# Local attention on one Trainium2 core: whole 128-token transposes replaced by pairs of 64-token ones that share two banks

## What is computed

```python
def attn_layer(x, Wqkv, qs, ksc, Wo):          # 16 heads of width 64, x is 2048 x 128
    q, k, v = heads of x @ Wqkv                # each 2048 x 1024
    q, k = l2norm(q) * qs, l2norm(k) * ksc
    q, k = rotary(q), rotary(k)
    out = local_attention(q, k, v)             # windows of 32 tokens see their own and the one before
    return out @ Wo
for i in range(6):
    x = attn_layer(shift_tokens(x), ...) + x
    x = ffn_layer(shift_tokens(x), ...) + x
```

## Time and profile before

| | |
|---|---|
| device time, median of 3 runs | 5310.74 us (5309.5 to 5312.04) |
| span of the profiled execution | 5297.4 us |
| median of the runs less that span | 13.3 us |
| PE busy, PE weight loads | 4675.9 us, 2897.7 us |
| DVE, ACT, POOL busy | 4003.6 us, 3636.0 us, 2657.4 us |
| mean granted TensorE clock | 0.957 |

### The profile page before, as it was taken

One profiled execution on the slowest core, in us unless ns is written; L12 is line 12 of the kernel. 1 busy time (PEld: TensorE's weight loads), 2 busy tenths in 40 slices (PEclk: granted clock), 3 DMA queues, 4 the chain that ended last, 5 costly groups with the idle time before them and its releaser, 6 DMA issues. The chain is left out here.

```text
span 5297.4 us, 148317 instructions
## 1 busy us (share of the span) xinstructions
PE 4675.9 (88%) x45796; PEld 2897.7 (55%) x45796; DVE 4003.6 (76%) x8097; ACT 3636.0 (69%) x11780; POOL 2657.4 (50%) x2108
## 2 busy tenths in 40 slices
PE   5999999698898998989989767989989989899897
PEld 1333332366565665656656544665656656566565
DVE  7888886587786877868778546878868778687785
ACT  1777777586785876858768514867858778587684
POOL 3000000465665666656656404656656566566564
PEclk6999999899999999999999977999999999999998
DMA  0000000222222222222222302222222222222223
GB/s 13 1 2 1 2 1 1 85 59 72 59 59 77 59 71 60 59 77 59 64 66 60 83 7 85 59 73 59 57 78 59 72 62 57 77 60 69 65 56 93
DMA packets 332305, 288.20 MB, mean 54 GB/s; under 512 B 149102, under 2 KB 290964, under 8 KB 329748
## 3 DMA queue, kind: packets, MB, share of 16 engines
q1 hardware_dynamic: 331028, 281.93, 20.6%
q10 hardware_dynamic: 768, 0.02, 0.0%
HBM read 100.42 MB, written 30.41 MB: 25 GB/s over the span
## 5 line engine op out<-in xcount | busy, mean ns | idle before, releaser
L929 POOL TENSOR_TENSOR g_rn<-g_ss,g_minus_half 128x8 f32<-128x8 f32 x384 | 636.8, 1658 | 299.7 <-DVE g_ss L1077 297.0
L929 POOL TENSOR_TENSOR f_rn<-f_ss,f_minus_half 128x8 f32<-128x8 f32 x384 | 636.8, 1658 | 299.2 <-DVE f_ss L1077 295.9
L425 DVE TENSOR_REDUCE a_maxima<-a_max 128x1 f32<-128x512 f32 x1024 | 651.3, 685 | 148.4 <-PE a_max L539 142.2
L1003 ACT ACTIVATE f_ex<-f_bank,f_nmx 128x96 f32<-128x96 f32 x1536 | 501.5, 338 | 226.8 <-DVE f_nmx L1082 226.8
L1003 ACT ACTIVATE g_ex<-g_bank,g_nmx 128x96 f32<-128x96 f32 x1536 | 501.6, 338 | 226.6 <-DVE g_nmx L1082 226.6
L349 ACT ACTIVATE a_pex<-a_scores 128x512 f32<-128x512 f32 x1024 | 531.7, 607 | 159.6 <-PE a_scores L548 159.6
L934 POOL TENSOR_TENSOR f_qr<-f_t 128x512 f32<-128x512 f32 x384 | 488.4, 1272 | 268.8 <-DVE f_t L1100 268.8
L934 POOL TENSOR_TENSOR g_qr<-g_t 128x512 f32<-128x512 f32 x384 | 488.2, 1271 | 269.0 <-DVE g_t L1100 269.0
L1172 PE MATMUL g_bank<-g_wqkv,g_xT 128*128 128x512 f32 x768 | 407.2, 613 | 30.4 <-ACT g_xT L977 24.3
L1172 PE MATMUL f_bank<-f_wqkv,f_xT 128*128 128x512 f32 x768 | 406.4, 612 | 29.2 <-ACT f_xT L977 24.5
L1077 DVE TENSOR_REDUCE g_ss<-g_sq 128x8 f32<-128x512 f32 x384 | 263.1, 685 | 207.9 <-ACT g_sq L985 207.9
(11 more groups left out here) (244 smaller groups left out, 11909.8 us busy)
## 6 DMA issues: line engine op xcount, KB each, us to landing
f_vw<-f_vt SPq DMA_DIRECT2D x96, 384.0 KB, 4.3
g_vw<-g_vt SPq DMA_DIRECT2D x96, 384.0 KB, 4.3
f_vw<-f_vt SPq DMA_DIRECT2D x96, 256.0 KB, 3.5
g_vw<-g_vt SPq DMA_DIRECT2D x96, 256.0 KB, 3.5
f_vw<-f_vt SPq DMA_DIRECT2D x96, 128.0 KB, 2.3
g_vw<-g_vt SPq DMA_DIRECT2D x96, 128.0 KB, 2.3
f_wqkv<-in_f_Wqkv_dram SPq DMA_DIRECT2D x7, 1536.0 KB, 9.5
g_wqkv<-in_f_Wqkv_dram SPq DMA_DIRECT2D x7, 1536.0 KB, 9.3
```

The costliest lines, as they stand in the source:

```text
L425: dve.tensor_reduce(maxima[:, m // 4, m % 4:m % 4 + 1], ps_max[m % 3][:], AX.X, ALU.max).then_inc(dv_max, 1)
L929: pool.tensor_tensor(rn[:, b, :], ss[:, b, :], minus_half[:], ALU.pow).then_inc(pl_rn, 1)
L1003: last = act.activation(ex[:, b, u, :], ps_s[:, h, KEYS * jj:KEYS * jj + KEYS], ACT.Exp, bias=nmx[:, b, u:u + 1], accum_out=sm[:, b, u:u + 1])
```

## The change

Each 128-token transpose becomes two of 64 tokens: one on the upper 64 rows of the array and one on the lower, with the 64x64 identity blocks. The two halves write to different banks. For that `ps_qkT` and `ps_pT`, till now one bank each, become two column halves of one pair of banks `ps_T`. Since TensorE then writes `ps_pT` in the banks from which ACT reads `ps_qkT`, and the other way round, PE has one more wait ahead of each of the two blocks. ACT's copies keep their size and read the pair of banks in another order. The order of the instructions on every engine is kept.

```diff
-        one = [bank(i) for i in range(6)]
+        one = [bank(i) for i in range(3)]
+        ps_T = bank(3, 2)
+        last_one = bank(5)
...
-        ps_qkT = banks[3]
-        ps_pT = banks[4]
+        ps_qkT = ps_T[:, :, 0:256]
+        ps_pT = ps_T[:, :, 256:512]
...
+        def made(t, c, lag):
+
+            return min(4 * t + c - lag, STEPS - 1) if isinstance(t, int) else 4 * t + c - lag
...
-                        act.copy(pT[0:KEYS, b, :, :], ps_pT[0:KEYS, :].rearrange("p (u q) -> p u q", u=4)).then_inc(act_pT, 1)
+                        act.copy(pT[0:KEYS, b, :, :].rearrange("p u (r q) -> p r u q", r=2),
+                                 ps_pT[0:KEYS].rearrange("p r (u q) -> p r u q", u=4)).then_inc(act_pT, 1)
...
-                            act.copy(qT[:, pairs, :], ps_qkT[:].rearrange("p (j q) -> p j q", j=4)).then_inc(act_qk, 1)
+                            act.copy(qT[:, pairs, :].rearrange("p j (r q) -> p r j q", r=2), turned).then_inc(act_qk, 1)
...
                         pe.wait_ge(dv_pn, upto(dv_pn, L, n - 6))
                         pe.wait_ge(act_pT, upto(act_pT, L, n - 7))
+                        pe.wait_ge(act_qk, upto(act_qk, L, made(t, c, 3))).then_inc(own["pe"], 1)
                         for u in range(4):
-                            last = pe.transpose(ps_pT[0:KEYS, P * u:P * u + P], pn[:, b, u, :], ident[:])
+                            for half in range(2):
+                                r = slice(BLK * half, BLK * half + BLK)
+                                last = pe.transpose(ps_pT[0:KEYS, half, BLK * u:BLK * u + BLK], pn[r, b, u, :], ident[r, r],
+                                                    tile_position=(BLK * half, 0))
                         last.then_inc(pe_pT, 1)
...
                         pe.wait_ge(pl_qr, upto(pl_qr, L, n - 2))
                         pe.wait_ge(act_qk, upto(act_qk, L, n - 3))
+                        pe.wait_ge(act_pT, upto(act_pT, L, made(t, c, 6))).then_inc(own["pe"], 1)
                         for j in range(4):
-                            last = pe.transpose(ps_qkT[:, P * j:P * j + P], qr[:, b, P * j:P * j + P], ident[:])
+                            for half in range(2):
+                                r = slice(BLK * half, BLK * half + BLK)
+                                last = pe.transpose(ps_qkT[:, half, BLK * j:BLK * j + BLK], qr[r, b, P * j:P * j + P], ident[r, r],
+                                                    tile_position=(BLK * half, 0))
                         last.then_inc(pe_qkT, 1)
```

More of the change, by code:

```diff
@@ L650, in bank @@
             return ctx.enter_context(nc.psum_tensor(f"{tag}_bank{i}", [P, n, 512], F32))
-        one = [bank(i) for i in range(6)]
+        one = [bank(i) for i in range(3)]
+        ps_T = bank(3, 2)
+        last_one = bank(5)
         ps_s = bank(6, 2)
-        banks = [t[:, 0, :] for t in one] + [ps_s[:, 0, :], ps_s[:, 1, :]]
+        banks = [t[:, 0, :] for t in one] + [ps_T[:, 0, :], ps_T[:, 1, :], last_one[:, 0, :], ps_s[:, 0, :], ps_s[:, 1, :]]
         ps_qk = banks[0:2]
         ps_v = banks[2]
-        ps_qkT = banks[3]
-        ps_pT = banks[4]
+        ps_qkT = ps_T[:, :, 0:256]
+        ps_pT = ps_T[:, :, 256:512]
         ps_o = banks[5]
@@ L738, in local_stack @@
         pe_s, dv_max, act_exp = sem("pe_s", STEPS, 4), sem("dv_max", STEPS), sem("act_exp", STEPS, 2)
-        dv_rd, dv_pn, pe_pT, act_pT = sem("dv_rd", STEPS), sem("dv_pn", STEPS, 2), sem("pe_pT", STEPS, 2), sem("act_pT", STEPS, 1)
+        dv_rd, dv_pn, pe_pT, act_pT = sem("dv_rd", STEPS), sem("dv_pn", STEPS, 2), sem("pe_pT", STEPS, 2), sem("act_pT", STEPS, 5)
         pe_o, act_aT = sem("pe_o", STEPS, 8), sem("act_aT", STEPS, 1)
@@ L1010, in tile @@
                         pairs = slice(4 * HALF[cj], 4 * HALF[cj] + 4)
+                        turned = ps_qkT.rearrange("p r (j q) -> p r j q", j=4)
                         act.wait_ge(pe_qkT, upto(pe_qkT, L, n - 2))
@@ L1017, in tile @@
                             act.wait_ge(act_kprev, upto(act_kprev, L, 2 * tj + HALF[cj]))
-                            act.copy(kT[:, pairs, WINDOW:], ps_qkT[:].rearrange("p (j q) -> p j q", j=4)).then_inc(act_qk, 1)
+                            act.copy(kT[:, pairs, WINDOW:].rearrange("p j (r q) -> p r j q", r=2), turned).then_inc(act_qk, 1)
                     if real(t, c, 7):
@@ L1257, in group @@
                     pe.wait_ge(act_qk, upto(act_qk, L, STEPS - 1))
+                    pe.wait_ge(act_pT, upto(act_pT, L, STEPS - 1))
                 if not known or m < NF:
```

## The result

The changed kernel takes 5725.68 us (median of 4 runs, 5725.14 to 5728.48) against 5310.12 us before (median of 4 runs, 5300.06 to 5312.04): a ratio of 1.0793, 95% interval 1.0778 to 1.0808. It is 415.6 us slower. The profiled executions have spans of 5724.0 and 5297.4 us, 426.6 apart.

What follows compares the result with a forecast made beforehand. PE, nearly gapless in attention, was taken to bound the kernel. The added wait makes a tile 18.81 us instead of 17.23; 180 tiles at 1.58 add 284 us to 5297.4, plus 13.3 around it: 5595 us, range 5450 to 5790.

Steps and rivals of the forecast that it cites:

- a ring: Loop from ps_qkT copy through pn transposes, scores, maximum and exponentials to the next copy: 18.81 us a tile, 1.58 more.
- The blocks: Transposes of pn and qr on PE: eight halves take 0.22 us against 0.44 whole, saving 1.76 us a tile.
- step 3: Tile's step with the output projection (c = 3): predicted 4.92 us copy to copy, 0.64 us shorter, the only one shrinking.
- the rival in which they don't: Halves of a transpose block don't run side by side: blocks of 0.44 us, kernel 5829 us; chance 0.15.
- The changes of tiling: PE pauses between blocks of different tiling: 0.10 us each, 11 more switches, 1.1 us a tile.
- The turns: Copy end to next copy end in the tile's steps c = 0 to 3: 4.77, 4.35, 4.77 and 4.92 us.
- the release: Delay from the end of ACT's ps_qkT copy to the start of PE's pn transposes: 0.08 us, between 0.05 and 0.12.
- From tile to kernel: Scaling the tile's 1.58 us loss by 15 tiles a layer, 6 layers, 2 stacks: 180 tiles, 284 us.
- The other wait: PE's added wait ahead of the qr transposes for the ps_pT copy of item n-6: costed at nothing.
- The copies' new order: ACT's copies from the shared banks, still 512 elements a row, read in another order: costed at nothing.
- The clock: Rival: gaps on PE lower the granted clock, a tenth of the attention at 1.2 GHz: 5815 us; chance 0.05.
- the main case: The late ps_qkT copy sets the tile's period while halved transposes overlap: 5595 us; chance 0.68.

Runs made afterwards that it cites:

- e1: Kernel before plus only the wait for the ps_qkT copy ahead of the whole pn transposes; no halves, no shared banks: 5777.93 us, ratio 1.0892.
- e3: Changed kernel, but from the third tile ACT's q/k copy reads the attention output's bank and the wait ahead of pn is dropped: 5427.24 us, ratio 1.0223.
- e6: Changed kernel with the transposes of qr whole again and only those of pn halved: 5713.98 us, ratio 1.0774.
- e7: Changed kernel with the transposes of pn whole again and only those of qr halved: 5784.66 us, ratio 1.0906.
- e2: Kernel before plus only the wait for the ps_pT copy ahead of the whole qr transposes: 5312.13 us, ratio 1.0008.
- e5: Changed kernel with shared banks and both waits kept, but whole transposes of both kinds, two to a bank: 5779.35 us, ratio 1.0898.

## Why the prediction was right, and where its sum was off

The direction, the mechanism and the place were right: the added wait ahead of the transposes of `pn` names a copy that ACT makes behind the exponentials, and closes a ring. e1 shows that it alone costs 8.9%, e3 that without it 1.74 of the 2.01 us that a steady tile had lost come back (19.29 to 17.55). The time of 5595 us was 131 us too low; the range of 5450 to 5790 holds the result. Point by point:

*The blocks.* Eight halves of `pn` were put at 0.22 us. They start 0.031 us apart, (0.43 - 0.216) / 7 with the record's own 0.216 us, 0.245 for eight, and L1188 to L1215 in step 3 takes 0.24. One after the other was put at 0.44, so they do run side by side; the rival in which they don't (5829 us) is out. A single record's row of the changed kernel:

```profile
L1188 PE MATMUL f_bank<-f_ident,f_pn x336: 216/216/260, 1401.2 to 1599.2; 64*96 64x64 f32 x168
```

*The changes of tiling.* The pause was put at 0.10 us. Block to next block is 0.36 us in the changed kernel, so 0.115 on top of 0.245: right. What was missing is the bare weight load. In the kernel before the weights of the v block, L1189, load from 1500.01, while the transposes ahead of it still run and 0.11 us before its matmul starts at 1500.12. In the changed kernel the weights of the same block, now L1201, start to load at 1507.29, at the same time as the matmul. PE's weight loads of before, then of after:

```profile
1500.01 0.30 PEld L1189 LDWEIGHTS f_bank<-f_wqkv,f_xT 128*128 128x128 f32 x2
```

```profile
1506.90 0.31 PEld L1188 LDWEIGHTS f_bank<-f_ident,f_pn 64*96 64x96 f32 x8 [1.74 <-issue]
1507.29 0.30 PEld L1201 LDWEIGHTS f_bank<-f_wqkv,f_xT 128*128 128x128 f32 x2
```

That is the 0.105 us per switch into an fp32 matmul that e6 and e7 place exactly. The hint stood in the earlier trace rows: four whole transposes took 0.49 us behind L1230, a switch, and 0.44 behind L1240, none. I read the 0.05 as a bound for the block and not as a weight load laid bare. With it PE's work does not shrink by 0.66 us a tile, as predicted, but grows, by 0.27 as e3 shows. This error of 0.93 us a tile cost the forecast little only because PE's work is not what bounds the changed kernel. The pause of 0.115 us agrees with the Trainium skill ("TensorEngine Tiling (Array Packing)", Key Properties), which says that a change of the tiling mode drains the engine. In these runs the pause is about half of what a switch into an fp32 matmul costs, 0.115 of 0.22 us.

*The turns*, predicted and measured: c = 0 4.77 and 4.98, c = 1 4.35 and 4.37, c = 2 4.77 and 4.84, c = 3 4.92 and 5.10 us. This is the term that was mis-sized, 18.81 for 19.29. In c = 0 and 2 there are 0.06 for the release (0.14, not 0.08), 0.04 for the block with its drain, and 0.10 for the bare load; in c = 1 the first two, and 0.05 for the bare load of the transpose of x. In c = 1 and 2 the maximum started 0.82 us behind the mask product and not 0.95, which gives 0.13 back. In c = 3 it is 0.06 for the release, 0.04 before L1242 and 0.08 until L1261 ends. That step did shrink, from 5.56, and is the only one that did. The release could have been read from the kernel before: there the mask product of step 3 waits for ACT's last exponential, which ends at 1512.07, and starts at 1512.22, 0.15 us behind it:

```profile
1512.22 0.26 PE L1203 MATMUL f_bank<-f_mask_bf,f_twice_bf 64*128 64x192 bf16 x2 [0.20 <-ACT f_ex L1003]
```

The 0.08 was an estimate that stood on no row.

*From tile to kernel.* The sum set out from 17.23 us, whose last period is the short one; from 17.28 it would have been 1.53 us more a tile and 9 us less in all. 180 tiles at 2.01 in place of 1.58 are 362 us; 77 of the 131 missing lie there. The other 54 lie at the ends of the layers, where I counted tiles and no more. From one layer to the next it was 339.4 us (1259.1 to 2956.2, five layers) and is 375.5 us, 36 more. Of these 24 are the twelve steady tiles, 6.5 the stretch up to the fourth transpose of x (36.9 to 43.4), and between 5 and 6 what follows the last transpose of x, up to the next layer's first. For the first of the two ends the three tiles counted there were nearly right (6.0 for 6.5); for the second no tile was counted. The load of the next layer's weights in the kernel before, then after:

```profile
L801 SPq MOVE f_wqkv<-in_f_Wqkv_dram x6: 29/29/29, 1259.1 to 2956.2; - x6
```

```profile
L807 SPq MOVE f_wqkv<-in_f_Wqkv_dram x6: 29/29/29, 1291.5 to 3169.2; - x6
```

*The other wait* was costed at nothing; e2 measures 0.08%, within what can be told. *The copies' new order* was costed at nothing; e5 equals e1.

*The clock.* In the steady stretch it stayed at 1.00, as the main case assumed, with PE busy 88% (some 84% were expected). At the start of a layer it is lower in both kernels. From the first transpose of x of the second layer to the fourth, before and after:

```profile
1327.70:1365.90 38.20, 30.01 (x199) 15.13 (x200) 25.06 (x46) 22.07 (x72) 24.33 (x16) 0.82 0.25 59
```

```profile
1362.80:1406.40 43.60, 31.72 (x243) 15.06 (x243) 26.48 (x47) 23.57 (x74) 24.77 (x17) 0.80 0.22 52
```

In the layers 3 to 6 the same stretch has 0.91, 0.91, 0.83 and 0.91 before, and 0.79, 0.82, 0.79 and 0.80 in the changed kernel. Over the whole execution the granted clock is 0.957 before and 0.943 now. Taken over the spans, 0.043 and 0.057 of them are 228 and 326 us. By this the lower clock costs about 98 us if PE's work bounds all stretches in which it is low, and less where PE waits (an estimate). It isn't the main cause: the profiled execution of e1 has 0.954, and e1 loses more than the changed kernel. How much of the 54 us it makes wasn't tried.

## What to carry to other kernels

Before two tensors are put into one bank, list who reads each and where that read stands in its engine's order: the shared bank makes the writer of one wait for the reader of the other, and if that read stands at the end of a chain which the writer's own next output starts, the wait closes a ring, and once its length exceeds the engine's own work it is the new period. A change of tiling in the array cost twice here, 0.115 us for the pause and 0.105 because the next block's first weights load in the open; halved blocks must save more than both, or stand beside a block of the same tiling. To find a ring's length, add the rows from a copy's end to the next copy's end, step by step; it gave each turn here to about 0.2 us.

## What the runs showed of the hardware

- After a change from 64-row tiles to the full array the first fp32 matmul's weights load only when the matmul starts (1507.29 for both): 697 ns for 592, and about 329 for 272 with a transpose. Behind a block of the same tiling the load starts 0.11 us ahead of the matmul (1500.01 for 1500.12) and the record has its 592 ns.
- 64-row fp32 transposes on alternating halves of the rows start 31 ns apart, whole ones about 110 ns apart (0.44 us for four): twice as many instructions in 0.55 of the time.
- PE started 0.14 us after the end of ACT's copy when a separate wait stood in between, in all four steps.
